# Weighing two key blocks at once in the narrow self attentions of a four-layer transformer kernel

## The reference, cut to what matters

```python
q, k, v = jnp.split(h @ Wqkv + bqkv, 3, axis=-1)       # 16 heads of 16
scores = jnp.einsum('bhnd,bhmd->bhnm', q, k) * 16 ** (-0.5)
p = jax.nn.softmax(scores, axis=-1)                     # over 1024 keys
o = jnp.einsum('bhnm,bhmd->bhnd', p, v)
x = x + o.transpose(0, 2, 1, 3).reshape(2, 1024, 256) @ Wos + bos
```

## Time and profile before

| what | us |
| --- | --- |
| median of 3 runs | 4588.85 (4585.59 to 4595.32) |
| span of the profiled execution | 4575.9 |
| TensorE busy | 4083.6 (89%) |
| VectorE busy | 3089.2 (68%) |
| ScalarE busy | 2075.6 (45%) |
| GpSimd busy | 1348.3 (29%) |

### The profile page before, as it was taken

One profiled execution on the slowest core, in us unless ns is written; L12 is line 12 of the kernel. 1 busy time (PEld: TensorE's weight loads), 2 busy tenths in 40 slices (PEclk: granted clock), 3 DMA queues, 4 the chain that ended last, 5 costly groups with the idle time before them and its releaser, 6 DMA issues.

```text
span 4575.9 us, 56543 instructions
## 1 busy us (share of the span) xinstructions
PE 4083.6 (89%) x20828; PEld 2493.2 (54%) x20828; DVE 3089.2 (68%) x4613; ACT 2075.6 (45%) x3756; POOL 1348.3 (29%) x664
## 2 busy tenths in 40 slices
PE   7999989789998887998999977888999999997889
PEld 5343346633334575555555546667555555546668
DVE  5888856688886666778777854345677777774355
ACT  2555544355565443444444435553344344444541
POOL 1100001100000124655655553421344444451120
PEclk8999989999998998999999988999999999998999
DMA  4223231123222333233223313223322232214220
GB/s 129 40 43 49 44 58 35 43 30 56 40 30 53 63 58 65 64 65 66 60 63 65 65 47 77 70 58 73 69 65 65 61 70 66 58 34 121 67 53 19
DMA packets 154420, 269.87 MB, mean 59 GB/s; under 512 B 36459, under 2 KB 70053, under 8 KB 153121
## 3 DMA queue, kind: packets, MB, share of 16 engines
q1 hardware_dynamic: 154144, 266.25, 27.7%
HBM read 105.01 MB, written 29.64 MB: 29 GB/s over the span
## 4 chain that ended last, share of the span: by engine, by line
PE 62%; DVE 16%; ACT 6%; issue 5%; POOL 4%; SPq 4%; DMA 3%; DVEq 0%; POOLq 0%; ACTq 0%
PE PS L1012 26%; PE PS L1191 12%; PE PS L1088 4%; PE PS L1084 4%; PE PS L1233 3%; PE PS L1321 3%; DVE t L1751 3%; PE PS L1243 2%; SPq L2181 2%; DVE t L1747 2%; POOL t L2042 1%; SPq L2198 1%; ACT t L1487 1%; DMA t<-t 1%; PE PS L1218 1%
## 5 line engine op out<-in xcount | busy, mean ns | idle before, releaser
L1012 PE MATMUL PS<-t 128*128 128x512 f32 (+4 forms) x7896 | 1981.4, 383 | 166.5 <-ACT t L1466 24.9
L1466 ACT ACTIVATE t<-PS 128x512 f32<-128x512 f32 (+2 forms) x1600 | 1166.6, 750 | 1175.6 <-PE PS L1012 1169.8
L1012 PEld LDWEIGHTS PS<-t 128*128 128x128 f32 (+2 forms) x7896 | 1246.0, 187 | 719.5 <-issue 260.2
L1191 PE MATMUL PS<-t 128*32 128x512 f32 (+2 forms) x4352 | 809.1, 610 | 0.2
L1747 DVE TENSOR_REDUCE t<-PS 128x1 fp32r<-128x1024 f32 x512 | 621.7, 1219 | 267.6 <-PE PS L1084 260.9
L1751 DVE TENSOR_REDUCE t<-PS 128x1 f32<-128x512 f32 x1024 | 650.8, 682 | 72.1 <-PE PS L1088 70.8
L2042 POOL TENSOR_TENSOR t<-t 128x1024 f32<-128x1024 f32 x256 | 617.6, 2412 | 130.4 <-ACT t L1466 103.4
L1088 PE MATMUL PS<-t 96*128 96x512 bf16 x1024 | 371.6, 395 | 33.9 <-DVE t L1751 14.8
L1084 PE MATMUL PS<-t 128*128 128x512 f32 x1024 | 338.6, 413 | 56.1 <-DVE t L1747 36.9
L2038 POOL TENSOR_TENSOR t<-t 128x1024 f32<-128x1024 f32 x64 | 155.1, 2424 | 747.5 <-PE PS L1201 448.7
L1191 PEld LDWEIGHTS PS<-t 128*32 128x32 f32 (+2 forms) x4352 | 170.6, 121 | 329.2 <-issue 324.5
(11 more groups left out here) (133 smaller groups left out, 3932.6 us busy)
## 6 DMA issues: line engine op xcount, KB each, us to landing
t<-t SPq DMA_DIRECT2D x640, 128.0 KB, 2.5
t<-scr_n SPq DMA_DIRECT2D x288, 128.0 KB, 6.5
t<-t SPq DMA_DIRECT2D x128, 256.0 KB, 3.9
scr_n<-t SPq DMA_DIRECT2D x72, 256.0 KB, 2.3
t<-t SPq DMA_DIRECT2D x256, 64.0 KB, 2.1
t<-in_L_Wg SPq DMA_DIRECT2D x16, 768.0 KB, 4.6
t<-in_L_W SPq DMA_DIRECT2D x36, 256.0 KB, 3.3
t<-in_L_Wo SPq DMA_DIRECT2D x64, 128.0 KB, 2.6
```

The costliest lines, as they stand in the source:

```text
L1012: ins = e.matmul(out, l, r, start=i == 0, stop=i == len(terms) - 1, tile_position=tp)
L1191: ins = e.matmul(banks[S.ot][wd * j:wd * j + wd, :], u.v[j][kt], P[0:S.pr, j, :], start=kt == 0, stop=kt == S.nkt - 1, tile_position=(0, w ...
L1466: e.activation(dst, src, ACT.Exp, scale=S.L.scale).then_inc(*expd.inc((S.i, i)))
```

## The change

In the two narrow self attentions `av` is put into the order only behind the scores of every second key block, and then weighs that block's two predecessors in one go: 16 instructions where there were twice 8. ScalarE's wait for a tile of probabilities names the odd block of the pair, since only that step signals now. The matmuls, their operands and the order of their sums stay; so do the three tiles, the three banks of the ring and everything in cross attentions, wide layers and MLPs.

```diff
@@ core_steps
             now = base + pr_n / places
-            if i >= 1:
+            if i >= 1 and (S.cross or i % 2 == 0):
                 an, akt = steps[i - 1]
                 plan.put(now, 0, [("av", S, an, akt)])
@@ tensor_program, av
                 w.wait_ge(expd, (S.i, (n * S.nkt + last) * 2 + 1))
-                kts = (last - 1, last) if S.L.style == 64 and not S.cross else (last,)
+                kts = (last,) if S.cross else (last - 1, last)
@@ scalar_program, score
                     else:
-                        w.wait_ge(weighed, (old.i, pn, pkt))
+                        w.wait_ge(weighed, (old.i, pn, pkt if old.cross else pkt | 1))
```

## The result

| what | before | after |
| --- | --- | --- |
| median (lowest to highest) | 4587.64 us (4585.59 to 4595.32), 4 runs | 4637.97 us (4632.15 to 4642.83), 4 runs |
| span of the profiled execution | 4575.9 | 4641.1 |

The ratio is 1.0101, 95% interval 1.0084 to 1.0119: the change costs 50 us. The profiled spans lie 65 us apart, more than the medians: the profiled execution of before is one of the quickest of that kernel, and that of after is the slowest of its four, 5 us above their median. Sizes of the whole are therefore read from medians, and the trace is used for single units.

A forecast was written before the change was run, and what follows sets the result against it. TensorE leads with VectorE close behind, coupled by the ring of three banks. (12.8 + 1.5) x 2 = 28.6 us added to the median 4588.85 gives 4617 us, 0.6% slower, range 4574 to 4645.

The forecast's parts named there:

- The hole in VectorE's supply: During a two-block weighing TensorE makes no maxima: 2.59 us until the next reduction, so VectorE stands about 0.83.
- TensorE alone decides: Rival for the narrow stages: VectorE's reserve suffices, waits stay, 29 us are saved, giving 4560; chance 0.17.
- bridged the single weighings: Ninth unit before the change: seven reductions ran through the weighing at 371.36 without a gap, so VectorE did not stand.
- The double weighing: Two key blocks weighed in 16 instructions on TensorE take 1.86 us, between 1.76 and 2.00.
- A merge saves: Joining two weighings on TensorE saves 0.14 plus 0.09 for one entry, 0.23 us; 29 us over 128 merges without more waiting.
- L1191's busy time: TensorE's weighing line in the narrow stages: busy time lower by some 15 us a stage.
- The replay of the ninth unit: Ninth unit's four stretches stepped through in the new order: +0.52, +0.26, +0.22 and -0.12, together 0.88 us longer.
- 0.85 a unit for all fifteen: Each of a layer's 15 units that make maxima gets 0.85 us longer, 12.8 us a layer.
- the rival of the wash: Longer units with norm and projection work gain in half their stretches, lose in half: 4589; chance 0.15.
- VectorE's norm work between reductions: In the first unit, norm statistics between reductions lengthen what bridges the gap, so the loss stays under 0.83 a merge.
- nothing else changed: Expected sign in the profile: besides weighing runs, busy time, waits and stages 14 us longer each, nothing differs.
- The last unit: It makes no maxima, but scores wait for ScalarE's exponentials: +1.5 us for the unit in each layer.

The follow-up runs named there:

- the pair: Changed kernel and kernel before, both with the layer-norm bias row's load issued behind the DMAs of the maximum rows: 4621.88 and 4590.12 us.
- the control: Kernel before with the layer-norm bias row's load issued behind the DMAs of the maximum rows: 4590.12 us, ratio 1.0001.
- the tenth experiment: Changed kernel with the last unit of each narrow self attention weighed one key block at a time again: 4636.54 us, ratio 1.0101.

## Why the prediction was right, and where its sizes were off

**Sign and mechanism: shown.** The forecast was 4617, the range 4574 to 4645, and 4637.97 lies in it, 21 us above the forecast. The hole in VectorE's supply is there behind each double weighing of the ninth unit, 0.87 to 1.10 us for the 0.83 of the text. Halving the reductions turns the sign in plain units and takes the cost off the whole; shortening them by a quarter makes plain units break even. That is the rival "TensorE alone decides" with its own condition: a reduction every 0.34 us is under the 0.5 that the text gave, and the saving is kept; at 0.46 to 0.49 a plain unit is within 0.2 us of nothing, and at 0.62 it loses. One part of the text was wrong all the same: VectorE had not bridged the single weighings, but stood behind most of them.

**The double weighing: right.** 1.86 us, as taken from the earlier trace rows. A merge saves 0.20 (0.79 in four), for 0.23. L1191's busy time fell by 21 us in all and not by 15 a stage: in the traces eight double weighings ran wholly or in part at half clock (up to 3.64 us for 1.92) and cost 9.5 us by that; before it was four single ones (up to 1.94 for 1.06), 3.5 us.

**The replay of the ninth unit: right.** Its stretches took 6.39, 6.78 and 7.27, forecast 6.45, 6.81 and 7.11; the one around `mturn` 8.39 (28.83 less the other three), forecast 8.31. The whole is 1.03 longer, for 0.88. The eighth is 1.04 longer, for 0.73. The 0.16 missed in the third stretch holds the wait of `norm`, 0.30, which the replay had not met.

**The step that failed: 0.85 a unit for all fifteen.** I replayed two plain units and carried them over. The table shows three kinds: plain units at 1.0; units with much other work (4, 5, 10, 15) at 0 to 0.4, as the rival of the wash had it; and units with a layer norm (1 to 3 and 11 to 13) at 1.2 to 3.9, with the fourteenth, 1.4, close to them. The text had supposed that VectorE's norm work between reductions helps to bridge the hole. In the thirteenth unit it does the opposite at `norm`, where it stands in front of a reduction that TensorE needs; the other norm units were not followed that far. The traces of the pair give 21 to 22 us a layer where 12.8 was written, and with the kernel before as the control 18 and 19. With the last units that makes 48 or 41 us, more than the medians' 32 for the whole. The profiled executions of the pair lie 55 us apart and their medians 32, so much of the excess is scatter between executions; the weighings that meet the lower clock in one execution and not in another are a part of it.

**The term that was missing: 16 us.** The collision of GpSimd's addition with VectorE's cast was nowhere in the prediction. It said "nothing else changed", yet the timing of GpSimd against VectorE did, with its order the same. The margin, an addition that began 1.1 us after a cast that it can hold up, stood in the trace of before, and so did a cast already held up, at 635.27; I did not look for either. Without the collision the measured 32 us stand beside the forecast 28.6. That this is so close is in part luck: plain units at 0.15 more than forecast, norm units at far more and other units at less happened to add up to about the same.

**The last unit: too small.** +1.5 was taken. To the end of its last weighing it is 2.36 longer in both layers (33.42 for 31.06), with the control as with the kernel before; 0.64 of that comes in its first two stretches. Weighed singly it is 0.63 longer in layer 0. So the text was right that this unit pays, and had its price too low.

**Of what should show it:** runs of 16 in 1.86 and the growing waits of L1088 came; VectorE's idle time grew by 21.7 us in layer 0's stage where 30 was written, for part of the standing had been there before. Up to the end of its fifteenth unit layer 0 is 23.5 us longer with the collision, for 14 with the last unit included.

**What stays open.** Why the merge with halved reductions did not give the 15 us or more expected is settled only for the plain units, the thirteenth and the last; units 1 to 3, 11 and 12 were not followed. That the shared ports hold the cast is inferred: it ends 0.28 or 0.29 us behind GpSimd's addition in three places, and with the addition moved away it takes its normal time. The two operations were not measured alone. In layer 0 of the tenth experiment's run it was the subtraction (L1652) that met the addition, and it took 5.00 us for 0.69.

## What to carry to other kernels

A longer run on the leading engine saves its switches, but the engine that it feeds gets nothing during the run beyond what the buffers hold. Set the run plus both latencies (here 2.59 us) against buffers times the consumer's pitch (three at 0.62) to see how long it will stand. Then ask whether it can catch up: with reductions every 0.34 us it stood longer, up to 1.75 us, and cost a plain unit nothing, since its work between two runs had become short. The price is what the leader waits for a buffer, not what the consumer stands, so replay both before counting the saving. Replay not one unit but each kind of unit, those above all where the consumer has other work queued in front of a buffer that the leader needs. And when an order shifts, look which GpSimd operations lie within a few microseconds of VectorE's casts in SBUF: moving one DMA issue was worth 16 us. In the kernel before, moving one small step behind a weighing was worth 37.

## What was unexpected of the hardware

A VectorE cast of 128x512 went from 0.42 to 3.34 and 4.73 us beside a GpSimd addition of 4.5 us (and to 4.62 at 635.27 of the kernel before), while reductions out of PSUM beside the same addition kept their 0.67. A stall of 4.29 us cost TensorE more than itself, for 5.4 us behind it ran at a granted clock of 0.50; and 1.59 us of waiting for a DMA was followed by a weighing at 0.53. The weighing of the changed kernel at 507.83 met the lower clock too, where TensorE had been idle between 501 and 507.5 for 0.21, 0.84 and 0.16 us only. Sixteen instructions in four column groups took exactly what eight in two groups do, 1.86 us.
